# Moving eight node units from the diffusion stage into the first layer's sums, and five sum places per turn instead of four

## The chip, the cores and the metric

One NeuronCore of a Trainium2 chip runs the whole program, a single launch. The metric is device time in microseconds, the median over executions. TensorE (PE) multiplies, VectorE (DVE), ScalarE (ACT) and GpSimd (POOL) do the rest; SyncE (SP), ACT and POOL issue the DMAs. POOL issues the gathers, that is DMAs whose rows in memory are picked by a list of indices.

## What is computed

Four graph layers in a row on 50000 nodes of 256 features and 12500 edges, each followed by a layer norm of input plus output:

```python
x = _layernorm(x + L0(x))   # two attention convolutions (GAT) with self loops
x = _layernorm(x + L1(x))   # graph transformer attention, only over edges
x = _layernorm(x + L2(x))   # gated message, out = agg + x, normed once more inside
x = _layernorm(x + L3(x))   # linear, silu, 6 steps of diffusion, linear

def _spmm(h, src, dst, inv_deg):
    return segment_sum(h[src], dst) * inv_deg[:, None]
for i in range(1, k + 1):             # k = 6
    term = _spmm(term, src, dst, inv_deg) / float(i)
    out = out + term
```

Only some nodes are the end of an edge. For all others the attention and message sums are empty, and the result of a node follows from its own row: a projection, norms, a linear layer with silu, a last linear layer and a norm. The kernel computes this *nodes' own path* for all 50000 nodes, in 196 units of 256 nodes, and the edge path overwrites the rows of the nodes that edges end in.

## The kernel before

**Edge path.** The edges are sorted by their end node and lie in T = 100 tiles of 128 slots. The stages follow one another: `project1`, `softmax`, `gat1`, `gather_out1`, `softmax`, `gat2`, `project_qkv`, `softmax`, `attend`, `mlp`, `diffuse`, `output`. Each opens a block in which every engine has a program of its own, and engines wait for one another by semaphores. Nothing schedules: the order in the code is the order on each engine.

**`gat1`, the first layer's sums.** It runs over 50 pairs of tiles. For each pair k, SP loads an equality matrix `b_equal` and two tiles `b_x` (four buffers), DVE multiplies them by the scores (`weigh`, L1474, two instructions), PE sums by matmul with the equality matrix (L1461), DVE adds (`join`, L1487) and ACT stores the result to `out1` in memory. DVE's order is `weigh(i)`, `join(i-1)`. Before pair 1 it does four long instructions of dot products (L1492, L1495). POOL issues 53 small gathers (`get_rep`, `rep_i`) in a row and then waits for the stage's end.

**`Dense`, the nodes' own path.** A turn works on up to six units at different stages. Its parts are, with the lag in units behind the newest one: `project` on PE (L801, lag 0), `add_c12` on DVE (L848, 0), `square_u` on ACT (L686, 0), `var_1` on DVE (L706, L707, 0), `pow_1` on POOL (L745, 0), `scales` on ACT (L692, 1), `scale_shift` on DVE (L713, L715, L718, 2), `var_3` (L725, L727, 2), `pow_3` on POOL (L750, 2), `third_norm` on DVE (L735, 2), `transpose` on PE (L678, 3), `move_x3` on ACT (L699, 3), `hidden` on PE (L810, 3), `silu` on ACT (L829, 4), `out_project` on PE (L819, 4), `add_out` on DVE (L855, L857, 4), `square_w` on ACT (L835, 5), `var_5` (L861, 5), `pow_5` on POOL (L868, 5), `last_norm` on ACT (L841, 5), load (L785) and store (L792) on SP. A stage with n units takes n + 5 turns. Within a turn each engine passes a few *gaps*, the same number on each engine, in which a stage puts work of its own. `PIECES`, the number of gaps, is 4.

**Where the units stand.** 36 units (`early`) run in `gather_out1` with tiles `m_...`; the other 160 run in `diffuse` with tiles `n_...`, in 165 turns with 660 gaps.

**`diffuse`.** Six steps of 100 sums and a closing one. `places` gives each step a sixth of the gaps and puts its 100 sums over all but the last nine of them, and the closing sum five gaps before the end. For a sum, POOL gathers 128 rows of `h` (`i_messages`, L620), eight sums ahead; PE multiplies by the equality matrix (L2558) in the sum's gap; DVE scales and adds (L2595) one gap later; SP stores the result to `h` two gaps later (five buffers `i_y`). After a step's last sum, SP loads the tiles' end rows (L2493), PE and DVE do the closing sum (L2554, L2589), POOL scatters it (L2526), and only then may POOL gather for the next step.

Of the kernel before, what the change touches and what calls it, by code (L numbers as in the profile page):

```python
# [90 lines left out]
class Net:  # L91
# [4 lines left out]
    def __init__(self, nc, a, ctx, edge_ctx):  # L96
# [3 lines left out]
        self.R = R = T * P  # L100
        self.early = 36
        self.H, self.DE = 8, a["edge_attr_t"].shape[0]
# [650 lines left out]
class Dense(Unmet):  # L753
# [117 lines left out]

    PIECES = 4

    def turn_sp(self, sp, j, u, gap):
        if v := self.at(j, u, -2):
            self.load(sp, *v)
        gap()
        gap()
        if v := self.at(j, u, 5):
            self.store(sp, *v)  # L880
        gap()
        gap()

    def turn_pe(self, pe, j, u, gap):
        if v := self.at(j, u, 0):
            self.project(pe, *v)
        gap()
        if v := self.at(j, u, 3):
            self.transpose(pe, *v)
        gap()  # L890
        if v := self.at(j, u, 4):
            self.out_project(pe, *v)
        gap()
        if v := self.at(j, u, 3):
            self.hidden(pe, *v)
        gap()

# [14 lines left out]
    def turn_dve(self, dve, j, u, gap):  # L912
# [14 lines left out]
        if v := self.at(j, u, 4):  # L927
            self.add_out(dve, *v)
        if third:
            self.third_norm(dve, *third)  # L930
        gap()

    def turn_gp(self, gp, j, u, gap):
        gap()
        gap()
        if v := self.at(j, u, 5):
            self.pow_5(gp, *v)
        if v := self.at(j, u, 2):
            self.pow_3(gp, *v)
        if v := self.at(j, u, 0):  # L940
            self.pow_1(gp, *v)
        gap()
        gap()
# [444 lines left out]
def gat1(net):  # L1388
# [7 lines left out]
    N = T // G  # L1396
    with Stage(nc) as st:
        EQ = st.sb("b_equal", [P, G, P], n=NB)
        X = st.sb("b_x", [P, G, 2, D], n=NB)
# [14 lines left out]
        block = st.ctx.enter_context(nc.Block())  # L1414

        @block.sync
        def _(sp):
            def load(k):
                if k < N:
# [3 lines left out]
                    sp.dma_start(X[k % NB][:, :, 0, :], tiles(net.out1[R:2 * R, :], k)).then_inc(x_in[k % NB], 16)  # L1423
                    sp.dma_start(X[k % NB][:, :, 1, :], net.proj_dst[k * G:(k + 1) * G, :, :].rearrange("g p d -> p g d")).then_inc(x_in[k % NB], 16)
            for k in range(N):
                load(k)

        @block.scalar
        def _(act):
            for k in range(N):  # L1430
                act.wait_ge(o_ready, k + 1)
                act.dma_start(net.ends[k * G:(k + 1) * G, :, :].rearrange("g r d -> r g d"), O[k % 3][0:2, :, :]).then_inc(ends_out[k % 3], 16)
                act.dma_start(tiles(net.out1, k), O[k % 3][:]).then_inc(stored[k % 3], 16)
            for u in range(3):
                act.wait_ge(ends_out[u], 16 * len(range(u, N, 3)))
# [3 lines left out]
        def _(gp):  # L1439
            for t in range(*net.ROWS):  # L1440
                get_rep(net, t).then_inc(reps_in, 16)
            gp.wait_ge(o_ready, N + 1)
# [8 lines left out]
        def _(pe):  # L1451
            for k in range(N + 1):
# [4 lines left out]
                else:  # L1457
                    pe.wait_ge(eq_in[k % NB], 16 * (k // NB + 1))
                    pe.wait_ge(msg_ready, k + 1)
                    for g in range(G):  # L1460
                        mm = nc.tensor.matmul(sums[k % 2][:, g * D:(g + 1) * D], EQ[k % NB][:, g, :], M[k % 2][:, g, 0, :], start=True, stop=True)  # L1461
                    mm.then_inc(summed, 1)

        @block.vector
        def _(dve):
# [30 lines left out]
            for i in range(1, N):  # L1496
                weigh(i)
                join(i - 1)
            join(N - 1)
            dve.wait_ge(reps_in, 16 * (net.ROWS[1] - net.ROWS[0]))  # L1500
# [4 lines left out]
def gather_out1(net):  # L1505
# [3 lines left out]
    with Stage(nc) as st:  # L1509
        dn = Dense(net, st.ctx, "m", 0, net.early)  # L1510
        dn.banks(*st.ps("m_bank", 4))
# [932 lines left out]
def diffuse(net):  # L2444
# [8 lines left out]
    with Stage(nc) as st:  # L2453
        dn = Dense(net, st.ctx, "n", net.early, Dense.all_units(net) - net.early)
        dn.banks(*st.ps("n_bank", 4))
# [362 lines left out]
```

## Time and profile before

| what | us |
|---|---|
| median of 3 runs (4128.31 to 4131.36) | 4131.34 |
| the profiled execution | 4160.81 |
| its span, first to last instruction | 4159.1 |
| its mean granted TensorE clock | 0.901 of full |

| engine | busy us | share |
|---|---|---|
| PE | 3324.5 | 80% |
| DVE | 2815.1 | 68% |
| POOL | 2545.2 | 61% |
| ACT | 1860.4 | 45% |

Busy time counts no instruction that only issues a DMA from SP or ACT, waits or branches. In this trace `gat1` runs from about 633 to 811 us, `gather_out1` from 811 to about 1120, `diffuse` from 2571 to about 3943. A line of the trace's order in time has start, duration, engine, line, operation, tiles (written <- read), shapes, how many instructions of one kind it merges, and in brackets how long the engine stood idle before it and what ended that. The names of tiles are the program's; the prefix `s_b_` is `gat1`, `m_` is `gather_out1`, `s_i_` and `n_` are `diffuse`.

### The profile page before, as it was taken

The numbers are of one execution on the slowest core, as the hardware profiler recorded it, in microseconds if no ns is written. First come the engines' busy times: TensorE is split into PE (matmuls) and PEld (weight loads), VectorE is DVE, ScalarE is ACT, GpSimd is POOL, SyncE is SP. The second block draws the span as 40 slices with busy tenths as digits, with TensorE's granted clock in tenths as the row PEclk, the third lists the DMA queues.
The fourth block names the chain that finished last, engine by engine and source line by source line (L and its number), as shares of the span: only waits on it lengthen the run. The fifth ranks groups of instructions, "written<-read, shape, count | busy, mean of one in ns | idle before, by whom it ended". The sixth has DMA issues, their size and how long they took to land. (4 is left out here: it accounts for less than half of the span.)

```text
span 4159.1 us, 57942 instructions
## 1 busy us (share of the span) xinstructions
PE 3324.5 (80%) x14668; PEld 2594.7 (62%) x14668; DVE 2815.1 (68%) x7889; ACT 1860.4 (45%) x5076; POOL 2545.2 (61%) x2930
## 2 busy tenths in 40 slices
PE   4999924568677699856999995499999999999775
PEld 3888712357455455433777774387878787878654
DVE  4666645559778455586666663488888888888732
ACT  2777700047523222223333331266656666666554
POOL 4777665188567566523333331487878787878667
PEclk8999955679899899955999997699999999999998
DMA  4877707724267322256333334976767676767664
GB/s 111 236 236 237 232 9 222 243 79 129 84 194 206 91 78 77 61 155 191 90 113 109 115 115 131 298 235 202 234 197 235 201 234 198 235 201 235 186 197 156
DMA packets 709256, 705.57 MB, mean 170 GB/s; under 512 B 92630, under 2 KB 663049, under 8 KB 708702
## 3 DMA queue, kind: packets, MB, share of 16 engines
q1 hardware_dynamic: 604546, 478.91, 37.5%
q0 software_dynamic: 74752, 181.57, 15.5%
q10 hardware_dynamic: 29660, 41.70, 3.0%
q8 instruction: 115, 1.88, 0.2%
q14 instruction: 183, 1.50, 0.1%
HBM read 422.60 MB, written 296.47 MB: 173 GB/s over the span
## 5 line engine op out<-in xcount | busy, mean ns | idle before, releaser
L620 POOL DMA_INDIRECT s_i_messages<-h,table_row x600 | 647.0, 1078 | 191.5 <-issue 129.7
L2558 PE MATMUL s_i_bank<-s_i_messages,s_i_equal 128*128 128x256 f32 x1200 | 364.5, 387 | 81.4 <-DMA s_i_messages<-h,table_row 76.8
L801 PE MATMUL s_n_bank<-w,n_xt 128*128 128x256 f32 x1280 | 308.0, 384 | 20.5 <-DMA n_xt<-in_x_t 20.5
L2595 DVE SCALAR_TENSOR_TENSOR s_i_y<-s_i_bank,s_i_scale,s_i_acc 128x256 f32<-128x256 f32 x600 | 284.6, 475 | 44.6 <-PE s_i_bank L2558 23.5
L819 PE MATMUL s_n_bank<-w_out,n_ht 128*128 128x256 f32 x1280 | 307.8, 384 | 0.9 <-ACT n_ht L829 0.9
L810 PE MATMUL s_n_bank<-n_x3t,w_in 128*128 128x256 f32 x1280 | 305.0, 381 | 0.0
L2558 PEld LDWEIGHTS s_i_bank<-s_i_messages,s_i_equal 128*128 128x128 f32 x1200 | 218.8, 193 | 112.7 <-issue 82.5
L841 ACT ACTIVATE n_w<-n_w,n_small 128x256 f32<-128x256 f32 x320 | 145.5, 502 | 313.0 <-POOL n_small L868 277.8
L801 PEld LDWEIGHTS s_n_bank<-w,n_xt 128*128 128x128 f32 x1280 | 247.2, 193 | 55.9 <-DMA n_xt<-in_x_t 20.9
L819 PEld LDWEIGHTS s_n_bank<-w_out,n_ht 128*128 128x128 f32 x1280 | 246.1, 193 | 35.6 <-ACT n_ht L829 1.3
L810 PEld LDWEIGHTS s_n_bank<-n_x3t,w_in 128*128 128x128 f32 x1280 | 244.6, 191 | 33.8 <-ACT n_x3t L699 0.2
L620 POOL DMA_INDIRECT s_e_x<-x,s_e_i x200 | 196.1, 981 | 111.0 <-issue 97.6
L620 POOL DMA_INDIRECT s_a_x<-in_x,index x200 | 200.2, 1001 | 64.2 <-issue 54.2
L735 DVE TENSOR_SCALAR n_x<-n_z,n_small 128x256 f32<-128x256 f32 x320 | 118.1, 409 | 121.4 <-POOL n_small L750 106.1
L2162 POOL TENSOR_TENSOR s_g_small<-s_g_small,neg_half 128x2 f32<-128x2 f32 (+1 forms) x51 | 43.7, 856 | 247.7 <-DVE s_g_small L2405 247.7
L686 ACT ACTIVATE n_squares<-n_u 128x256 f32<-128x256 f32 x320 | 130.6, 410 | 143.2 <-DVE n_u L848 79.1
L745 POOL TENSOR_TENSOR n_small<-n_small,neg_half 128x4 f32<-128x4 f32 x160 | 165.0, 1031 | 42.4 <-DVE n_small L707 42.4
L1855 PE MATMUL s_e_ps_qv<-w_qv,s_e_xt 128*128 128x512 f32 x400 | 189.9, 597 | 0.0
L692 ACT ACTIVATE n_z<-gamma_bc,n_small 128x256 f32<-128x256 f32 x320 | 173.3, 591 | 13.7 <-POOL n_small L745 13.7
L1461 PE MATMUL s_b_sums<-s_b_messages,s_b_equal 128*128 128x256 f32 x200 | 87.9, 586 | 106.1 <-DVE s_b_messages L1474 82.7
L2397 DVE SCALAR_TENSOR_TENSOR s_g_y<-s_g_x,real,s_g_bank 128x512 f32<-128x512 f32 x50 | 37.4, 747 | 184.1 <-PE s_g_bank L2253 184.1
L868 POOL TENSOR_TENSOR n_small<-n_small,neg_half 128x2 f32<-128x2 f32 x160 | 116.5, 728 | 72.2 <-DVE n_small L861 68.7
(422 smaller groups left out, 9436.1 us busy)
## 6 DMA issues: line engine op xcount, KB each, us to landing
h<-s_i_y SPq DMA_DIRECT2D x600, 128.0 KB
n_xt<-in_x_t SPq DMA_DIRECT2D x160, 256.0 KB
out<-n_w SPq DMA_DIRECT2D x160, 256.0 KB
s_i_equal<-eq_tab SPq DMA_DIRECT2D x600, 64.0 KB
x<-s_x_rows SPq DMA_DIRECT2D x100, 256.0 KB
out<-s_a_hs SPq DMA_DIRECT2D x100, 128.0 KB
proj_dst<-s_a_hd SPq DMA_DIRECT2D x100, 128.0 KB
h<-s_h_rows SPq DMA_DIRECT2D x50, 256.0 KB
```

What stands on the lines that cost most here:

```text
L620: return net.nc.gpsimd.indirect_dma_start(out, None, table, bass.IndirectOffsetOnAxis(index, 0))
L686: sq = self.nc.scalar.activation(self.squares[0][:, g, :], self.U[u][:, g, :], ACT.Square, scale=self.D ** -0.5, accum_out=self.S[u][:, g: ...
L692: sc = self.nc.scalar.activation(self.Z[u][:, g, :], self.net.bc["gamma"][:], ACT.Identity, bias=self.S[u][:, self.POWERED + g:self.POWERE ...
L735: nm = self.nc.vector.tensor_scalar(self.X3[u][:, g, :], self.Z[u][:, g, :], s[:, 24 + 2 * g:25 + 2 * g], s[:, 32 + g:33 + g], ALU.subtrac ...
L745: self.nc.gpsimd.tensor_tensor(self.S[u][:, first:first + n], self.S[u][:, 8 - n:8], self.net.neg_half[:, 0:n], ALU.pow).then_inc(self.sca ...
L801: mm = self.nc.tensor.matmul(self.pr[:, g * self.D:(g + 1) * self.D], self.XT[u][:, c, g * P:(g + 1) * P], self.net.w12[:, c, :], start=c ...
L810: mm = self.nc.tensor.matmul(self.hd[:, 2 * m * P:2 * (m + 1) * P], self.net.w_in[:, c, m * P:(m + 1) * P], self.X3T[:, c, :], start=c == ...
L819: mm = self.nc.tensor.matmul(self.op[:, g * self.D:(g + 1) * self.D], self.HT[:, m, g * P:(g + 1) * P], self.net.w_out[:, m, :], start=m = ...
L841: nm = self.nc.scalar.activation(self.W[u][:, g, :], self.W[u][:, g, :], ACT.Copy, scale=self.S[u][:, 40 + g:41 + g])
L1855: nc.tensor.matmul(qvs[b][:, :], XT[b][:, c, :], net.w_qv[:, c, :], start=c == 0, stop=c == C - 1)
L2558: nc.tensor.matmul(banks[r % 4][:, 0:D], EQ[q % NM][:], M[q % NM][:], start=True, stop=True).then_inc(summed, 1)
L2595: V.scalar_tensor_tensor(Y[q % NY][:], banks[r % 4][:, 0:D], scale[:, s, t:t + 1], acc[:, t, :], ALU.mult, ALU.add).then_inc(added, 1)
```

## The change

Eight units become a third `Dense` with tiles `l_...` in `gat1`; `gather_out1` keeps its 36 and starts with unit 8; `diffuse` keeps 152, in 157 turns. `PIECES` becomes 5, so `diffuse` has 785 gaps and `gather_out1` 205 instead of 164. In `gat1` the 13 turns of the eight units stand behind every third pair, k = 0, 3, ..., 36, and the 53 small gathers on POOL are split into 13 chunks, one ahead of each turn.

```diff
-        self.early = 36
+        self.first_units, self.early = 8, 36
...
-    PIECES = 4
+    PIECES = 5
...  # turn_pe: a second gap behind hidden
             self.hidden(pe, *v)
+        gap()
         gap()
...  # turn_dve: a gap between add_out and third_norm
             self.add_out(dve, *v)
+        gap()
         if third:
             self.third_norm(dve, *third)
...  # turn_gp and turn_sp: a third gap at their end
+        gap()
         gap()
         gap()
...  # gat1
+        dn = Dense(net, st.ctx, "l", 0, net.first_units)
+        dn.banks(*st.ps("l_bank", 4))
+        TURNS = dn.units + 5
+        EVERY = (N - 1) // TURNS
...
+        def turn_at(k):
+
+            i = k // EVERY
+            return (i // 2, i % 2) if k % EVERY == 0 and 0 <= i < TURNS else None
...  # SP
             for k in range(N):
                 load(k)
+                if v := turn_at(k - 3):
+                    dn.turn_sp(sp, *v, none)
...  # ACT, behind the two stores of pair k
+                if v := turn_at(k):
+                    dn.turn_act(act, *v)
...  # POOL
-            for t in range(*net.ROWS):
-                get_rep(net, t).then_inc(reps_in, 16)
+            t0, t1 = net.ROWS
+            at = lambda i: t0 + min(i, TURNS) * (t1 - t0) // TURNS
+            for i in range(TURNS):
+                for t in range(at(i), at(i + 1)):
+                    get_rep(net, t).then_inc(reps_in, 16)
+                dn.turn_gp(gp, i // 2, i % 2, none)
...  # PE, behind the matmuls of pair k
+                    if v := turn_at(k):
+                        dn.turn_pe(pe, *v, none)
...  # DVE
                 weigh(i)
                 join(i - 1)
+                if v := turn_at(i - 1):
+                    dn.turn_dve(dve, *v, none)
...
-        dn = Dense(net, st.ctx, "m", 0, net.early)
+        dn = Dense(net, st.ctx, "m", net.first_units, net.early)
...
-        dn = Dense(net, st.ctx, "n", net.early, Dense.all_units(net) - net.early)
+        dn = Dense(net, st.ctx, "n", net.first_units + net.early, Dense.all_units(net) - net.first_units - net.early)
```

What that moves, first on DVE in `gat1`. `s4_b_...` are the stage's own tiles. Before, the two kinds of instruction alternate from the dot products to the end:

```order
L1495 TENSOR_REDUCE dots2<-s4_b_products 128x200
L1474 TENSOR_TENSOR s4_b_messages1<-s4_b_x1,scores_1 128x512 x2
L1487 TENSOR_TENSOR s4_b_out0<-s4_b_sums0,s4_b_messages0 128x512
L1474 TENSOR_TENSOR s4_b_messages0<-s4_b_x2,scores_1 128x512 x2
L1487 TENSOR_TENSOR s4_b_out1<-s4_b_sums1,s4_b_messages1 128x512
```

After, on DVE in the middle of the stage:

```order
L1517 TENSOR_TENSOR s4_b_out0<-s4_b_sums1,s4_b_messages1 128x512
L713 TENSOR_TENSOR l_z1<-l_u1,l_z1 128x512
L715 TENSOR_TENSOR l_z1<-l_z1,beta_bc 128x512
L718 BN_STATS l_small1<-l_z1 128x6 x2
L848 TENSOR_TENSOR l_u1<-s4_l_bank0,c12 128x512
L861 TENSOR_SCALAR l_small0<-l_small0 128x2
L725 BN_AGGR l_small1<-l_small1 128x2 x2
L727 TENSOR_SCALAR l_small1<-l_small1 128x2
L706 TENSOR_SCALAR l_small1<-l_small1 128x2
L707 TENSOR_SCALAR l_small1<-l_small1 128x2
L855 TENSOR_TENSOR l_w1<-s4_l_bank3,l_x31 128x512
L857 TENSOR_TENSOR l_w1<-l_w1,b_out_bc 128x512
```

A whole turn now stands behind the addition of every third pair (the last of it, L735, follows these rows), and the next pair's multiplication stands behind the turn.

On DVE in `diffuse`, the end of one turn and the start of the next, before:

```order
L2595 SCALAR_TENSOR_TENSOR s12_i_y1<-s12_i_bank0,s12_i_scale,s12_i_acc 128x256
L855 TENSOR_TENSOR n_w0<-s12_n_bank3,n_x30 128x512
L857 TENSOR_TENSOR n_w0<-n_w0,b_out_bc 128x512
L735 TENSOR_SCALAR n_x30<-n_z0,n_small0 128x256 x2
L2595 SCALAR_TENSOR_TENSOR s12_i_y2<-s12_i_bank1,s12_i_scale,s12_i_acc 128x256
L713 TENSOR_TENSOR n_z1<-n_u1,n_z1 128x512
```

After, in a turn whose place between L857 and L735 is one of those without a sum:

```order
L2627 SCALAR_TENSOR_TENSOR s12_i_y2<-s12_i_bank3,s12_i_scale,s12_i_acc 128x256
L855 TENSOR_TENSOR n_w1<-s12_n_bank3,n_x31 128x512
L857 TENSOR_TENSOR n_w1<-n_w1,b_out_bc 128x512
L735 TENSOR_SCALAR n_x31<-n_z1,n_small1 128x256 x2
L2627 SCALAR_TENSOR_TENSOR s12_i_y3<-s12_i_bank0,s12_i_scale,s12_i_acc 128x256
L713 TENSOR_TENSOR n_z0<-n_u0,n_z0 128x512
```

Most turns still hold four sums; which of the five places stays empty wanders through the turn.

## Rows read from the trace of the kernel before

**Rows 1.** Busy time by stretch: us, busy (count) by engine, granted clock, DMA share, GB/s.

```profile
706.00:800.00 94.00, 59.71 (x134) 34.58 (x134) 65.36 (x108) 0.00 (x0) 0.18 (x1) 0.65 0.96 318
...
2680.00:3930.00 1250.00, 1174.76 (x5562) 994.59 (x5561) 1076.63 (x2941) 769.32 (x2351) 1006.98 (x1052) 0.99 0.72 219
```

**Rows 2.** Groups on POOL, 2680 to 3930: busy us, mean ns | idle before, releasers.

```profile
L620 POOL DMA_INDIRECT s_i_messages<-h,table_row x575 | 621.9, 1081 | 167.0 <-issue 123.5 <-DVE n_small L727 28.1 <-DMA h<-s_i_bound,bound_row 10.2
L745 POOL TENSOR_TENSOR n_small<-n_small,neg_half 128x4 f32<-128x4 f32 x156 | 160.9, 1031 | 0.0
L868 POOL TENSOR_TENSOR n_small<-n_small,neg_half 128x2 f32<-128x2 f32 x158 | 115.1, 728 | 68.7 <-DVE n_small L861 65.3
```

**Rows 3.** POOL in order of time, one turn of the diffusion with four sums.

```profile
3100.81 0.72 POOL L868 TENSOR_TENSOR n_small<-n_small,neg_half 128x2 f32<-128x2 f32 x1
...
3103.38 1.50 POOL L620 DMA_INDIRECT s_i_messages<-h,table_row  x1 [0.18 <-issue]
3105.19 0.96 POOL L620 DMA_INDIRECT s_i_messages<-h,table_row  x1 [0.31 <-issue]
3106.45 0.95 POOL L620 DMA_INDIRECT s_i_messages<-h,table_row  x1 [0.30 <-issue]
...
3108.69 0.72 POOL L868 TENSOR_TENSOR n_small<-n_small,neg_half 128x2 f32<-128x2 f32 x1
```

**Rows 4.** PE in order of time: a sum in that turn, and neighbours without sums.

```profile
3103.54 0.60 PE L2558 MATMUL s_i_bank<-s_i_messages,s_i_equal 128*128 128x256 f32 x2
3103.97 1.89 PE L819 MATMUL s_n_bank<-w_out,n_ht 128*128 128x256 f32 x8
...
2847.11 1.89 PE L810 MATMUL s_n_bank<-n_x3t,w_in 128*128 128x256 f32 x8
2848.83 0.38 PE L801 MATMUL s_n_bank<-w,n_xt 128*128 128x256 f32 x1
```

**Rows 5.** DVE in order of time, the end of that turn.

```profile
3102.26 0.73 DVE L735 TENSOR_SCALAR n_x<-n_z,n_small 128x256 f32<-128x256 f32 x2 [0.66 <-POOL n_small L750]
3102.91 0.48 DVE L2595 SCALAR_TENSOR_TENSOR s_i_y<-s_i_bank,s_i_scale,s_i_acc 128x256 f32<-128x256 f32 x1
3103.30 0.68 DVE L713 TENSOR_TENSOR n_z<-n_u,n_z 128x512 f32<-128x512 f32 x1
```

**Rows 6.** POOL in order of time: the first gather of a new step.

```profile
2852.24 1.00 POOL L620 DMA_INDIRECT s_i_messages<-h,table_row  x1 [2.00 <-DMA h<-s_i_bound,bound_row]
```

**Rows 7.** Groups on DVE in `gat1`, 633 to 800.

```profile
L1474 DVE TENSOR_TENSOR s_b_messages<-s_b_x,scores 128x512 f32<-128x512 f32 x100 | 64.9, 690 | 66.1 <-DMA s_b_x<-proj_dst 61.2 <-issue 3.6
L1487 DVE TENSOR_TENSOR s_b_out<-s_b_sums,s_b_messages 128x512 f32<-128x512 f32 x50 | 34.3, 686 | 26.1 <-DMA proj_dst<-s_a_hd 14.6 <-PE s_b_sums L1461 11.5
L1495 DVE TENSOR_REDUCE dots<-s_b_products 128x200 f32<-128x1600 f32 x2 | 5.7, 2856 | 0.1
L1492 DVE TENSOR_TENSOR s_b_products<-scores 128x1600 f32<-128x1600 f32 x2 | 3.6, 1822 | 0.0
```

**Rows 8.** DVE in order of time in `gat1`: the first pair, a long wait, the last pair.

```profile
637.61 1.29 DVE L1474 TENSOR_TENSOR s_b_messages<-s_b_x,scores 128x512 f32<-128x512 f32 x2 [41.65 <-DMA s_b_x<-proj_dst]
...
705.10 0.69 DVE L1487 TENSOR_TENSOR s_b_out<-s_b_sums,s_b_messages 128x512 f32<-128x512 f32 x1 [7.29 <-DMA proj_dst<-s_a_hd]
...
793.05 0.69 DVE L1487 TENSOR_TENSOR s_b_out<-s_b_sums,s_b_messages 128x512 f32<-128x512 f32 x1 [1.63 <-PE s_b_sums L1461]
```

**Rows 9.** ACT in order of time, one turn of the diffusion.

```profile
3110.26 0.82 ACT L829 ACTIVATE n_ht<-s_n_bank,cols 128x256 f32<-128x256 f32 x2
3111.61 0.60 ACT L699 ACTIVATE n_x3t<-s_n_bank 128x512 f32<-128x512 f32 x1 [0.53 <-PE s_n_bank L678]
3112.11 1.08 ACT L692 ACTIVATE n_z<-gamma_bc,n_small 128x256 f32<-128x256 f32 x2
3113.09 0.41 ACT L835 ACTIVATE n_squares<-n_w 128x256 f32<-128x256 f32 x1
...
3114.39 0.42 ACT L686 ACTIVATE n_squares<-n_u 128x256 f32<-128x256 f32 x1 [0.40 <-issue]
```

**Rows 10.** PE in `gather_out1`, in order of time, after an idle stretch of 5.72 us.

```profile
895.10 3.62 PE L819 MATMUL s_m_bank<-w_out,m_ht 128*128 128x256 f32 x8
```

More of the change, by code:

```diff
@@ L941, in turn_gp @@
             self.pow_1(gp, *v)
+        gap()
         gap()
@@ L1414, in gat1, with none @@
         block = st.ctx.enter_context(nc.Block())
+        def none():
+            pass
+        def turn_at(k):
+            i = k // EVERY
+            return (i // 2, i % 2) if k % EVERY == 0 and 0 <= i < TURNS else None
         @block.sync
@@ L1424, in load @@
                     sp.dma_start(X[k % NB][:, :, 1, :], net.proj_dst[k * G:(k + 1) * G, :, :].rearrange("g p d -> p g d")).then_inc(x_in[k % NB], 16)
+            for u in range(2):
+                dn.load(sp, 0, u)
             for k in range(N):
                 load(k)
+                if v := turn_at(k - 3):
+                    dn.turn_sp(sp, *v, none)
+            for u in range(2):
+                sp.wait_ge(dn.stored[u], 16 * (dn.units // 2))
         @block.scalar
```

## The prediction

> **What bounds the kernel now.** I read busy time by stretch first, then who waits for whom in the two stages that change, then single turns in order of time.
>
> In the middle of the diffusion PE is busy for 1174.76 of 1250 us, at clock 0.99 [rows 1]. That looks like the bound, and it is not, since matmul records overlap. Matmul groups L810 and L801 that follow each other without a sum start 1.73 us apart, and a sum takes 0.43 (3103.54 to 3103.97) [rows 4]. With four sums and transposes that take about as long as a sum, PE needs 3 x 1.73 + 5 x 0.43 = 7.35 us a turn. The turn takes 7.88 (3100.81 to 3108.69) [rows 3].
>
> POOL is full there. Each gather starts 1.26 after the one before (3105.19 to 3106.45), and the 0.30 between them is ended by nothing but issue [rows 3]. Four gathers are 5.04 us; what is left of the turn, 2.84, goes to the three powers and to a first gather that takes 1.50 instead of 0.95 [rows 3]. DVE waits 0.66 for POOL ahead of L735 [rows 5]. Over the stretch POOL idles beyond issue for about 68.7 + 10.2 us, nearly all between steps [rows 2]. So POOL sets the turn, and a turn costs 1.26 per gather plus 2.84.
>
> In `gat1` nothing of this holds: DMA is busy for 0.96 at 318 GB/s, POOL for 0.18 us of 94, and the clock is 0.65 [rows 1]. DVE has the longest chain, from 637.61 to 793.05 plus 0.69, 156 us [rows 8]. Of these 64.9 + 34.3 + 5.7 + 3.6 = 108.5 are work [rows 7], and 47.5 are waits, mostly for loads and stores; the longest, up to 7.29 each, fall while the 53 small gathers run [rows 8].
>
> **The diffusion, part by part.** Eight turns go. The 600 gathers stay, so what POOL saves is 8 x 2.84 = 22.7 us, and not eight whole turns of 7.88 (63 us). Five places only let the same sums stand in fewer turns: 100 sums over 121 or 122 gaps are 4.1 a turn. POOL then needs 4.1 x 1.26 + 2.84 = 8.0, PE 5.62 + 4.1 x 0.43 = 7.4; POOL stays the bound.
>
> The new place ahead of L735 stands in DVE's wait: an addition occupies 0.39 (3102.91 to 3103.30) of 0.66 [rows 5], so it costs nothing. If that cover were gone it would cost at most 0.39 in each of some 146 turns (six steps of 24.4), 57 us.
>
> Between steps, POOL may gather again only when the closing sum is scattered (2.00 us of wait at the end of that chain [rows 6]). Seven gaps lie between the last sum and the scatter. They are 1.75 turns before and 1.4 after, 0.35 x 5.6 = 2 us less if the turn sets them, nothing if the DMAs do. About half, 1 us at each of five boundaries: -5. The first 100 us of the stage (bulk loads) and its last turns wait for DMAs; I leave them as they are.
>
> What a first gather of 1.50 costs beyond 0.95 coincides with L713, which starts at 3103.30, while the gather starts at 3103.38 [rows 3, 5]. In turns whose last place is empty (about one in five), L713 starts 0.39 earlier and the overlap shrinks: 146 / 5 x 0.35 = 10 us at most, nothing at least; I take -1. Sum for the diffusion: -22.7 - 5 - 1 = -29; bounds -23 and -43 (and +28 if the cover were gone).
>
> The Trainium skill ("SBUF — State Buffer", Who interferes with whom) says that a DVE instruction with two SBUF inputs contends with a GpSimd instruction that reads SBUF, and that order of issue decides who blocks. L713 has two such inputs and the row of 1.50 agrees. By that rule alone, the empty last place would shift the block to the power L745 in part, and the sum would be -28 instead of -29.
>
> **`gat1`, part by part.** The added work on DVE is that of eight units. In the diffusion a turn of DVE takes 7.88 less 0.66 of wait less four additions of 0.39, 5.66. Eight of them are 45 us. That is the least it can cost if nothing is waited for inside a turn, and if all of it went into the 47.5 of waits, the stage would take no longer at all.
>
> I do not expect that, since here the turn stands between two pairs, and its parts wait for one another across engines. ACT starts its turn when the pair is joined and its two stores are issued (0.73 after). Then it does silu, 0.8, `move_x3`, 0.5, `scales`, 0.98, `square_w`, 1.0 or more, `square_u`, 0.94; starts of these are 3110.26, 3111.61, 3112.11, 3113.09 and 3114.39 [rows 9]. `var_1` on DVE needs the last and stands ahead of L855, L857 and L735 (2 x 0.72 + 0.73). So DVE's turn takes 0.73 + 4.3 + 0.2 + 2.2 = 7.4 after the pair, of which 1.7 is wait for ACT. Three turns of thirteen have all parts. The others by the same chain with the parts that they have: 3.0, 2.9, 4.7, 5.1, 6.3 ahead of them and 6.9, 5.9, 4.6, 4.2, 1.9 behind. All thirteen: 22.2 + 22.0 + 23.5 = 68 us.
>
> PE adds to that while its clock is low. A group of eight records took 3.62 instead of 1.89 in `gather_out1` behind an idle stretch of 5.72 [rows 4, 10]. PE's turn at 1.2 GHz would be 11.2 us instead of 5.6, and the next pair's sum stands behind it: up to 4 us more a turn, 10 turns, 40. At full clock nothing. The stage's 0.65 lies near 1.2 GHz, but a turn fills PE for over 5 us; I take 9 us. The Trainium skill ("TensorE: Matmul & The Clock Gate", Part 1) has the clock go to full once PE has been busy for a while and back when it idles. This speaks for the smaller value; by it the sum would be 3 to 5 us lower.
>
> Waits for DMA: the 13 pairs behind the last turn still run at the DMA's pace, 94 us for some 38 pairs or 2.45 each against 1.98 of work, 6 us. In a turn SP stands at the unit's store until `last_norm`, and the loads of the fourth pair ahead are queued behind it; these land about when DVE wants them, so 0 to 1 us in eight turns, 4. The long waits during the small gathers go, since those now come in fours.
>
> DVE's chain: 108.5 + 68 + 9 + 10 = 195.5 against 156, **+39**; bounds +5 and +75.
>
> `gather_out1`: same units, same turns, same gathers. Its 40 small gathers fill 8 turns instead of 10, POOL-bound in both; 0, between -3 and +3.
>
> Profiled execution: 4160.8 + 39 - 29 + 2 (the stage waits for the last unit store at its end, which no row shows) = 4172.8. The median of the runs is 29.5 us below the profiled execution. I carry the difference over: 4131.3 + 12 = **4143**.
>
> **The rivals.** (a) *The units fill the waits.* If ACT and PE run far enough ahead, DVE's turn costs its 5.66 and takes the place of the DMA waits: 108.5 + 45 + 12 = 166, +10. With -29 and +2 this is 4114. For it: 47.5 us of waits and idle ACT, POOL. Against: ACT's part can't start before the join. It decides as soon as a full turn on DVE is under 6.2 us. (b) *The diffusion gets no shorter*, because something other than POOL binds at five places: the five `i_y` buffers come back too late, or PE does. Then -7 instead of -29: 4165. Against: PE has 0.5 us of room a turn. (c) *`gat1` stays at 1.2 GHz*, or SP's store starves the loads: +69 instead of +39, 4173. (d) *The first gather's stall goes away in all turns*, since DVE's order changed. Then PE binds at 7.4 to 7.8 in some 80 turns: some 25 us more, 4118. Against: the distance from L745 to L713 changes in one turn of five alone.
>
> **How the numbers follow.** Forecast 0.56, own range 4130 to 4158. (a) 0.16, (b) 0.10, (c) 0.10, (d) 0.08. A measurement of this kernel tells a change from none at about 0.2%, 8.3 us, so from 4123.1 to 4139.6 counts as the same. The forecast's lower part lies there: 0.16 of its 0.56, and 0.40 slower. (a) gives 0.13 faster and 0.03 same, (d) 0.05 and 0.03; (b) and (c) are slower. Faster 0.18, same 0.22, slower 0.60. The range takes in (a), (d) and most of (b) and (c): 4112 to 4173.
>
> **What would show it.** In the diffusion: step period 4 to 5 us shorter, a turn with four sums still 7.9, POOL's gathers still ended by issue alone, DVE's wait ahead of L735 near 0.3 where its new place is filled. In `gat1`: DVE's chain near 195, a full turn near 7.4 with waits for ACT ahead of L861 and L706, waits for loads under 15 us in all. Clock above 0.65. The prediction falls if a full turn on DVE is near 5.7 (a), if the step period stays (b), if PE's records there are mostly over 0.6 us (c), or if four-sum turns are 7.4 (d).

## The result, and the profile after

| | before | after |
|---|---|---|
| median, us | 4129.83 (4 runs, 4127.78 to 4131.36) | 4160.80 (4 runs, 4158.44 to 4164.26) |
| the profiled execution, us | 4160.81 | 4158.44 |
| `gat1` with `project1` ahead of it, start to start | 751.0 | 783.2 |
| `gather_out1` | 332.8 | 336.2 |
| `diffuse` | 1379.9 | 1353.2 |

The changed kernel is slower: ratio 1.0076 with an interval of 1.0059 to 1.0093, +31 us. The forecast was 4143, +12. The profiled executions differ by -2.4 us only. So the traces and the medians don't tell the same story, and most of what follows is about that.

Busy time by stretch of the kernel after (columns as in [rows 1]):

```profile
706.00:800.00 94.00, 63.45 (x215) 46.30 (x213) 64.57 (x127) 24.11 (x73) 43.05 (x42) 0.81 0.75 238
2680.00:3930.00 1250.00, 1156.30 (x5410) 977.02 (x5411) 1047.62 (x2861) 736.18 (x2252) 992.11 (x1039) 0.98 0.74 221
```

In `gat1` the clock rose from 0.65 to 0.81, and DMA fell from 0.96 to 0.75: the stage is no longer at the pace of its transfers. Now DVE in order of time: the first pair, a turn with all its parts at pair 21, and the last pair.

```profile
631.91 1.29 DVE L1504 TENSOR_TENSOR s_b_messages<-s_b_x,scores 128x512 f32<-128x512 f32 x2 [47.22 <-DMA s_b_x<-proj_dst]
...
722.46 0.69 DVE L1517 TENSOR_TENSOR s_b_out<-s_b_sums,s_b_messages 128x512 f32<-128x512 f32 x1
...
725.87 0.69 DVE L848 TENSOR_TENSOR l_u<-s_l_bank,c 128x512 f32<-128x512 f32 x1 [0.61 <-PE s_l_bank L801]
729.02 0.17 DVE L861 TENSOR_SCALAR l_small<-l_small 128x2 f32<-128x2 f32 x1 [2.46 <-ACT l_squares L835]
...
731.94 1.28 DVE L1504 TENSOR_TENSOR s_b_messages<-s_b_x,scores 128x512 f32<-128x512 f32 x2
733.14 0.68 DVE L1517 TENSOR_TENSOR s_b_out<-s_b_sums,s_b_messages 128x512 f32<-128x512 f32 x1
...
825.86 0.69 DVE L1517 TENSOR_TENSOR s_b_out<-s_b_sums,s_b_messages 128x512 f32<-128x512 f32 x1 [1.63 <-PE s_b_sums L1489]
```

The chain that [rows 8] show as 156 us long is 825.86 + 0.69 - 631.91 = 194.6 us; forecast 195.5. A pair without a turn takes 2.0 us from one L1517 to the next; from pair 21 to 22 it is 733.14 - 722.46 = 10.68, so this turn costs 8.7. The two other turns with all parts (pairs 15 and 18) cost 6.8 and 6.7. The three make 7.4 on average, the number of the forecast, but that 7.4 was for full clock, with PE's slow clock as a surcharge of its own; at full clock the turn is 6.8, so 0.6 less than forecast. Pair 21 is dearer because PE ran it at 1.2 GHz (granted clock 0.50 from 722 to 726): its L801 group took 3.62 us instead of 1.89, and DVE waited for it at L848, and for ACT, which had waited for PE, at L861. PE in order of time:

```profile
722.21 3.62 PE L801 MATMUL s_l_bank<-w,l_xt 128*128 128x256 f32 x8
```

What DVE waited for in the whole stage, in groups (window 600 to 850, so L1504 includes the 47.22 ahead of the first pair):

```profile
L1504 DVE TENSOR_TENSOR s_b_messages<-s_b_x,scores 128x512 f32<-128x512 f32 x100 | 64.7, 688 | 61.1 <-DMA s_b_x<-proj_dst 58.4
L1517 DVE TENSOR_TENSOR s_b_out<-s_b_sums,s_b_messages 128x512 f32<-128x512 f32 x50 | 34.3, 686 | 3.0 <-PE s_b_sums L1489 2.9
L855 DVE TENSOR_TENSOR l_w<-s_l_bank,l_x 128x512 f32<-128x512 f32 x8 | 5.5, 688 | 5.8 <-PE s_l_bank L819 5.8
L861 DVE TENSOR_SCALAR l_small<-l_small 128x2 f32<-128x2 f32 x8 | 1.4, 170 | 14.9 <-ACT l_squares L835 14.9
L706 DVE TENSOR_SCALAR l_small<-l_small 128x2 f32<-128x2 f32 x8 | 1.4, 170 | 6.3 <-ACT l_squares L686 6.3
```

Behind the first pair 61.1 - 47.2 = 13.9 us of waits for loads are left, where [rows 7] had 66.1 - 41.7 = 24.4 and another 26.1 ahead of the additions. In their place stand 14.9 + 6.3 for ACT and 5.8 for PE inside the turns.

In the diffusion, POOL in order of time, a turn with four sums:

```profile
3123.45 1.00 POOL L745 TENSOR_TENSOR n_small<-n_small,neg_half 128x4 f32<-128x4 f32 x1
3124.63 1.50 POOL L620 DMA_INDIRECT s_i_messages<-h,table_row  x1 [0.18 <-PE s_i_bank L2590]
3126.43 0.95 POOL L620 DMA_INDIRECT s_i_messages<-h,table_row  x1 [0.30 <-issue]
3127.70 0.95 POOL L620 DMA_INDIRECT s_i_messages<-h,table_row  x1 [0.30 <-issue]
3128.95 0.96 POOL L620 DMA_INDIRECT s_i_messages<-h,table_row  x1 [0.30 <-DVE n_small L727]
...
3132.50 1.50 POOL L620 DMA_INDIRECT s_i_messages<-h,table_row  x1 [0.18 <-issue]
```

The turn takes 3132.50 - 3124.63 = 7.87 (7.88 in [rows 3]), and the gathers are still 1.25 to 1.27 apart. From the middle of one step to that of the next it is 214.4 us instead of 218.8, mean of five: 4.4 shorter.

### The profile page after: what moved, and what is told of

Same layout as the page of the kernel before. It is cut to its first block and busy times, and to the rows that moved or that the text cites. A ratio compares the mean times of both kernels' runs of the same rounds, so it can differ in the third digit from the quotient of the medians.

```text
span 4156.7 us, 57935 instructions
## 1 busy us (share of the span) xinstructions
PE 3314.6 (80%) x14668; PEld 2598.4 (63%) x14668; DVE 2812.0 (68%) x7889; ACT 1857.7 (45%) x5076; POOL 2540.2 (61%) x2930
## 5 line engine op out<-in xcount | busy, mean ns | idle before, releaser
L620 POOL DMA_INDIRECT s_i_messages<-h,table_row x600 | 633.8, 1056 | 196.0 <-issue 104.2
L2590 PE MATMUL s_i_bank<-s_i_messages,s_i_equal 128*128 128x256 f32 x1200 | 351.9, 389 | 76.0 <-DMA s_i_messages<-h,table_row 71.5
L801 PE MATMUL s_n_bank<-w,n_xt 128*128 128x256 f32 x1216 | 296.6, 388 | 20.6 <-DMA n_xt<-in_x_t 20.6
L819 PE MATMUL s_n_bank<-w_out,n_ht 128*128 128x256 f32 x1216 | 296.0, 388 | 0.1
L810 PE MATMUL s_n_bank<-n_x3t,w_in 128*128 128x256 f32 x1216 | 289.3, 381 | 0.3 <-ACT n_x3t L699 0.3
L801 PEld LDWEIGHTS s_n_bank<-w,n_xt 128*128 128x128 f32 x1216 | 237.2, 195 | 55.5 <-DMA n_xt<-in_x_t 21.1
L620 POOL DMA_INDIRECT s_e_x<-x,s_e_i x200 | 193.6, 968 | 110.9 <-POOL s_e_i L1866 78.7
L819 PEld LDWEIGHTS s_n_bank<-w_out,n_ht 128*128 128x128 f32 x1216 | 234.4, 195 | 32.6 <-ACT n_ht L829 0.5
L810 PEld LDWEIGHTS s_n_bank<-n_x3t,w_in 128*128 128x128 f32 x1216 | 232.8, 192 | 33.0 <-ACT n_x3t L699 0.7
L620 POOL DMA_INDIRECT s_a_x<-in_x,index x200 | 195.8, 979 | 64.7 <-issue 55.9
L735 DVE TENSOR_SCALAR n_x<-n_z,n_small 128x256 f32<-128x256 f32 x304 | 112.1, 409 | 115.8 <-POOL n_small L750 115.8
L745 POOL TENSOR_TENSOR n_small<-n_small,neg_half 128x4 f32<-128x4 f32 x152 | 155.0, 1020 | 45.9 <-DVE n_small L707 45.9
L620 POOL DMA_INDIRECT s_d_x<-in_x,index x100 | 98.4, 984 | 95.5 <-DVE s_d_y L1817 48.4
L868 POOL TENSOR_TENSOR n_small<-n_small,neg_half 128x2 f32<-128x2 f32 x152 | 116.8, 769 | 60.8 <-DVE n_small L861 57.5
```

What stands on the lines that cost most here:

```text
L620: return net.nc.gpsimd.indirect_dma_start(out, None, table, bass.IndirectOffsetOnAxis(index, 0))
L745: self.nc.gpsimd.tensor_tensor(self.S[u][:, first:first + n], self.S[u][:, 8 - n:8], self.net.neg_half[:, 0:n], ALU.pow).then_inc(self.sca ...
L801: mm = self.nc.tensor.matmul(self.pr[:, g * self.D:(g + 1) * self.D], self.XT[u][:, c, g * P:(g + 1) * P], self.net.w12[:, c, :], start=c ...
L810: mm = self.nc.tensor.matmul(self.hd[:, 2 * m * P:2 * (m + 1) * P], self.net.w_in[:, c, m * P:(m + 1) * P], self.X3T[:, c, :], start=c == ...
L819: mm = self.nc.tensor.matmul(self.op[:, g * self.D:(g + 1) * self.D], self.HT[:, m, g * P:(g + 1) * P], self.net.w_out[:, m, :], start=m = ...
L868: self.nc.gpsimd.tensor_tensor(s[:, 40:42], s[:, 38:40], self.net.neg_half[:, 0:2], ALU.pow).then_inc(self.dev5, 1)
```

## The experiments

The runs fell on several chips, and these are of two kinds for this program: on some the kernel before takes 4125 to 4131 us (medians), on two others 4156 ("at 4155" below), at about the same granted clock (0.895 to 0.910 in all runs). Each chip was used on one occasion only, so whether the chip or the occasion makes the difference isn't shown; "chip" stands for both. The result above is of the first kind. Each ratio below is against the kernel before on the same chip. By "the chain of `gat1`" I mean the time from the first multiplication to the end of the last addition on DVE, as above.

Where the expectations number their theories: theory 1 says that the long waits of `gat1` in [rows 8] are not in the executions that were timed; the others are told where they stand.

### The kernel before, once more (chip at 4155)

> The kernel before, unchanged, profiled a second time. Question: the first profiled execution was 29.5 us over the median of the plain runs, the profiled execution of the changed kernel is not. Theory 1 (the long waits in gat1 beside the small gathers are not there in every execution): this one comes out near 4130 us, gat1 near 130 to 140 us on DVE instead of 156. Theory 2 (the excess is spread over all stages): near 4130 with gat1 still at 156, and each other stage a little shorter. Theory 3 (a profile of this kernel costs 30 us): again 4160.

Profiled execution 4161.43, medians of its neighbours 4155.68. The chain of `gat1` is 158.0 us, and the long waits are there as in [rows 8] (up to 10.5 us from one addition to the next). Here the profile agrees with the medians, so "the profiler makes it 30 us longer" falls. It says nothing on the chips of the other kind.

### The parts of the change, one at a time (chip at 4155)

`gat1` alone; the eight units are computed there and a second time in the old place:

```diff
-        self.early = 36
+        self.first_units, self.early = 8, 36
...  # gat1 as in the changed kernel; m and n units and PIECES as before
```

> The kernel before, with the eight units in gat1 as in the changed kernel, while gather_out1 keeps units 0 to 35 and diffuse the other 160 (so eight units are computed twice) and PIECES stays 4. It prices gat1's part alone. My sum: +39 us, bounds +5 to +75. Theory 1 of b_again (timed runs have a shorter gat1 than the profile showed): +55 to +60. Rival (the units fill waits): +10.

Ratio 1.0085 (1.0066 to 1.0105), +35 us; `gat1` is 41.9 us longer in the trace. Near the forecast of +39.

The five places alone:

```diff
-    PIECES = 4
+    PIECES = 5
...  # and the gaps in turn_pe, turn_dve, turn_gp, turn_sp
```

> The kernel before with five places in a turn and no unit moved: 165 turns in diffuse, 825 gaps. It prices the places alone. POOL-bound: each turn costs 2.84 plus 1.26 a gather whatever the places, so the time changes by what the step's ends save, 0 to -5 us. Rival (the DVE or PE order costs or gains by itself): beyond -15 or +15.

Ratio 0.9996 (0.9983 to 1.0010): nothing. The steps are 218.7 us long, as before. So the places themselves neither help nor cost in sum, and the -5 for the step ends isn't seen in the time. Inside, things move all the same: over the 500 gathers from the middle of the first step to the middle of the last, POOL's gathers are 17 us shorter than before and its three powers 21 us longer, in 138 turns instead of 137.

The changed kernel with `gat1` as before; units 0 to 7 are computed nowhere, so this kernel leaves out the own path of 2048 nodes (chip at 4155):

```diff
-        dn = Dense(net, st.ctx, "l", 0, net.first_units)
...  # and its turns; the 53 small gathers in a row again
```

> The changed kernel with gat1 as before: units 0 to 7 are computed nowhere, diffuse has 152 units and five places. It leaves out eight units, so it prices what diffuse gets back in timed runs. My sum: -29 us (POOL 8 x 2.84 plus the step ends). If each unit were worth a whole turn: -63. If the diffusion got no shorter: 0 to -7.

Ratio 0.9935 (0.9909 to 0.9960), -27 us, with an interval from -38 to -17. In the traces `diffuse` alone is 23.6 us shorter. This is what the diffusion gives, and the sum said -29.

### The changed kernel on a chip at 4155

> The changed kernel, unchanged, beside the kernel before on the chip of these runs. If the parts simply add, gat1 +35 to +40 (e_gat1_units_only) and diffuse -26 (the two profiles), it comes to +10 to +15 us. If the first result holds on any chip, +24 to +38.

4170.91 (11 runs) against 4155.66 (23 runs): ratio 1.0037 (1.0023 to 1.0051), **+15 us**, near the forecast +12, and not the +31 of the result. The chain of `gat1` is 195.3 us, so it is as long as on the other kind of chip. The changed kernel is 10 us slower here than in the result, the kernel before 26; what makes the two differences unequal must lie in the kernel before.

### Does POOL set the turns of the diffusion?

```diff
         # pow_5
+        self.nc.gpsimd.tensor_tensor(s[:, 44:46], s[:, 38:40], self.net.neg_half[:, 0:2], ALU.pow)
```

> The changed kernel with pow_5 on POOL done twice in every turn, the first into unused columns. If POOL sets the diffusion's turns, a turn gets 0.7 us longer wherever POOL is full: 0.7 x about 135 turns of diffuse, +95 us, step period 214 to 230. If PE sets them, POOL's extra work is hidden: +0 to +15.

POOL in order of time (L869 is the second power):

```profile
3118.87 0.73 POOL L868 TENSOR_TENSOR n_small<-n_small,neg_half 128x2 f32<-128x2 f32 x1
3119.58 0.69 POOL L869 TENSOR_TENSOR n_small<-n_small,neg_half 128x2 f32<-128x2 f32 x1
...
3122.09 1.51 POOL L620 DMA_INDIRECT s_i_messages<-h,table_row  x1 [0.18 <-issue]
...
3130.61 1.50 POOL L620 DMA_INDIRECT s_i_messages<-h,table_row  x1 [0.18 <-issue]
```

A turn is 3130.61 - 3122.09 = 8.52 instead of 7.87: the added 0.69 comes through nearly whole. Steps are 230.8 us long, the diffusion is 92.4 us longer than in the changed kernel on that chip, and `gather_out1` 14.9. This is one execution, 4287.66: +117 against the median of the changed kernel, +108 against its profiled execution. The +95 expected is met by the diffusion alone. POOL is the bound there, though PE is busy for 92% of the middle of the stage. In `gather_out1` its 41 turns would make 28 us if all came through, and about half did, so POOL sets only a part of that stage.

### What a turn in `gat1` costs

The next pair's multiplication is put into the turn, behind `scale_shift`, where DVE otherwise waits for ACT:

```diff
+                    def gap():
+                        nonlocal weighed
+                        if next(n) == 0 and i + 1 < N:
+                            weigh(i + 1)
+                            weighed = i + 1
-                    dn.turn_dve(dve, *v, none)
+                    dn.turn_dve(dve, *v, gap)
```

> The changed kernel with one thing moved: in gat1 DVE does the next pair's weigh (1.3 us) inside the turn, behind scale_shift, instead of behind the turn, so that it fills the wait for ACT ahead of var_5 and var_1. Theory (a full turn costs 7.4 or more because DVE waits for ACT and PE inside it): 1.0 to 1.3 us less in each of eleven turns, -11 to -15 us against a_again. Rival (gat1 is bound by loads or by SP's stores): no change against a_again, waits for loads take the place.

Ratio 1.0033 (1.0015 to 1.0050), the same as the changed kernel on that chip, where 11 to 15 us less were expected. The edit did what it should, and its groups on DVE (window 633 to 845) show what took its place:

```profile
L1504 DVE TENSOR_TENSOR s_b_messages<-s_b_x,scores 128x512 f32<-128x512 f32 x100 | 64.6, 688 | 69.4 <-DMA s_b_x<-proj_dst 67.1
...
L861 DVE TENSOR_SCALAR l_small<-l_small 128x2 f32<-128x2 f32 x8 | 1.3, 166 | 1.1 <-ACT l_squares L835 0.9
```

The wait for ACT at L861 fell from 14.5 us (the changed kernel on that chip) to 1.1. But the waits for loads behind the first pair grew from 58.6 - 44.3 = 14.3 to 69.4 - 44.3 = 25.1. The chain is 193.0 instead of 195.3. Why the loads are late is in SyncE's waits; here those of the changed kernel in the first run (columns: who waited <- for whom: us in total, times, longest):

```profile
SPq L792 <- ACT l_w L841: 55.9, 8, 9.6
SPq L1437 <- PE s_b_sums L1489: 31.1, 19, 5.8
```

SP stands in the stores of the eight units (L792) for 55.9 us, and the loads for the pairs are queued behind them. Two kernels take that away, the second with the edit above too (chip at 4125):

```diff
-                if v := turn_at(k - 3):
+                if v := turn_at(k - 4):
                     dn.turn_sp(sp, *v, none)
```

> The changed kernel with one edit: in the first layer's sums SP does its part of a turn (a unit's load and the store of a finished unit) one pair later, that is behind the loads of the fourth pair ahead and not ahead of them. Nothing else moves. In the trace of the changed kernel SP stands for 54 us in eight such stores, up to 8.6 us each, with the loads queued behind them; DVE waits about 14 us for loads behind the first pair. Theory (DVE's turn with its waits for ACT sets the pace, the loads come second): the waits for loads fall by some 5 us, gat1 is 0 to 6 us shorter, the time 0 to 6 us below the changed kernel, that is 9 to 15 us above the kernel before. Rival (SP's stores starve the loads, and that is most of what a turn costs): 14 us or more below the changed kernel.

> Both edits: the next pair's multiplication stands inside the turn on DVE, and SP's part of the turn stands one pair later. With the first edit alone a turn became 1 to 1.5 us shorter in the trace, yet waits for loads grew from about 14 to 25 us and the time did not move. Theory (the gain of the first edit was given back as waits for loads, because SP stands in the unit's store with the loads queued behind it): now waits for loads fall back to about 10 us, gat1 is some 12 to 16 us shorter than in the changed kernel, the time -1 to +5 us against the kernel before. Rival (the loads are late because the DMA engines are full and not because SP issues them late): waits for loads stay near 25, the time stays near +14.

The store alone: ratio 1.0076 (1.0061 to 1.0091), which is what the changed kernel had in the result, on a chip of this kind; waits for loads behind the first pair 9.7 us, chain 193.6. Both edits: 1.0050 (1.0035 to 1.0065), 10 us less on the same chip; the waits for loads are 13.0 where the first edit alone had 25.1, the one at L861 is 3.4, the chain is 185.2. So the two waits cover each other, and only taking both away pays. The changed kernel itself was not run on this chip, and each single edit on one kind only, so this rests on ratios from several chips; on one chip alone it is shown that the multiplication inside the turn gives 10 us once the store is moved, and on another that it gives nothing without that. The absolute numbers of both expectations are missed: the store alone +32.7 against the kernel before where 9 to 15 were expected, both +22.5 where it was -1 to +5, since on this kind of chip the changed kernel starts from +31; I had carried +15 over. Against the changed kernel `gat1`'s chain is 9 us shorter with both edits, where 12 to 16 were expected.

### The long waits of `gat1` without the units

The kernel before, with the small gathers in 13 chunks, each behind the sums of every third pair:

```diff
-            for t in range(*net.ROWS):
-                get_rep(net, t).then_inc(reps_in, 16)
+            for i in range(13):
+                gp.wait_ge(summed, 3 * i + 1)
+                for t in range(t0 + i * (t1 - t0) // 13, t0 + (i + 1) * (t1 - t0) // 13):
+                    get_rep(net, t).then_inc(reps_in, 16)
```

> The kernel before, with the 53 small gathers of gat1 in 13 chunks, each waiting for the sum of every third pair, and no unit. If the small gathers cause gat1's long waits in the timed runs, -15 to -25 us. If the timed runs have no such waits, 0 within 0.2%.

On the chip at 4155: 4137.79, ratio 0.9960 (0.9944 to 0.9975), **-17 us**, the chain 136.7 instead of 158.0. This beats both kernels there. The changed kernel has this pacing in it as a side effect, so there its +15 hides a gain of some 17 in `gat1`. Then the same again, with a trace of the kernel before, on a chip that gave 4125.94:

> The kernel before, unchanged, once more, with its trace. Its median was 4130 where the changed kernel came out 31 us slower, 4125 on a third occasion, and 4155 where the changed kernel was only 15 us slower; both of its traces so far (4161 each) are of the slower kind. Chips differ, and the question is which stage of the kernel before is shorter on a quicker one. Theory 1: where the kernel before runs at 4125 to 4131, its long waits in gat1 (up to 9 to 11 us between additions while the 53 small gathers run) are missing, so gat1 ends some 15 us earlier behind its first pair, at about 125 to 130 us from the first to the last addition instead of 144. Rival: the waits are there as ever (143 to 146 us), and the difference of 30 us lies in the stages that read and write whole tables (project1 458 instead of 467, mlp and others). Where the chip gives about 4155 again, this run tells nothing new.

> The kernel before with the 53 small gathers of gat1 in 13 chunks, each behind the sums of every third pair, as in the run that came out 17 us quicker, on the same chip as the look at the kernel before. Where the chip gives the kernel before about 4155: again 13 to 20 us quicker. Where it gives 4125 to 4131: by theory 1 within 5 us of the kernel before, since the waits that the pacing takes away aren't there; by the rival 13 to 20 us quicker as well, about 4110.

Paced: 4124.34 (12 runs) against 4125.94 (17 runs), ratio 0.9996 (0.9984 to 1.0007). Nothing left to gain, and the trace of the kernel before says why. Busy time by stretch, first before on the chip at 4155 (the first repetition), then before on this one:

```profile
675.00:712.00 37.00, 10.77 (x21) 6.37 (x22) 10.60 (x17) 0.00 (x0) 23.93 (x25) 0.50 0.46 138
```

```profile
675.00:698.00 23.00, 15.89 (x37) 9.53 (x36) 17.00 (x27) 0.00 (x0) 17.88 (x17) 0.65 1.10 366
675.00:712.00 37.00, 25.74 (x59) 15.06 (x57) 27.85 (x45) 0.00 (x0) 18.82 (x18) 0.66 1.10 368
```

In the first the DMA engines are busy for 0.46 at 138 GB/s and DVE for 10.60 us; on the second they run at 1.10 and 368 GB/s. There the small gathers end at 698 already, but until then POOL issues them at the same pace, and the DMA engines move 366 GB/s beside them. In order of time, all engines, first a long wait of the first:

```profile
699.15 1.29 DVE L1474 TENSOR_TENSOR s_b_messages<-s_b_x,scores 128x512 f32<-128x512 f32 x2
...
700.59 2.05 PE L1461 MATMUL s_b_sums<-s_b_messages,s_b_equal 128*128 128x256 f32 x4 [7.06 <-issue]
...
708.85 0.36 SPq L1421 DMA_DIRECT2D s_b_equal<-eq_tab  x1
708.86 0.69 DVE L1487 TENSOR_TENSOR s_b_out<-s_b_sums,s_b_messages 128x512 f32<-128x512 f32 x1 [8.41 <-DMA proj_dst<-s_a_hd]
```

The name in the bracket misleads: `proj_dst<-s_a_hd` is a store of `project1`, the last of which was issued at 514.6. SP's load L1421 waits for nothing but PE's sum, and it and the addition start together. The semaphore that PE raises at the end of the sum goes up at 708.83, 6.8 us after the start of the pair's last matmul (702.01); in a pair without a long wait it takes 0.65. So what DVE, and SP with it, waits for here is PE's sum being reported as done. It is so in each of the four traces with long waits, wherever the semaphore is recorded: up to 7.6 us instead of 0.65, and the addition starts 0.03 later. And the transfers aren't what is slow. The loads issued by 699.27 have landed by 702.61, and then the DMA engines have next to nothing to do until SP issues again:

```profile
702.70:708.80 6.10, 0.00 (x0) 0.00 (x0) 0.00 (x0) 0.00 (x0) 2.83 (x3) 0.50 0.05 11
```

Now the ends of the chain of the second, where no addition is more than 3.0 us behind the one before it:

```profile
626.98 1.29 DVE L1474 TENSOR_TENSOR s_b_messages<-s_b_x,scores 128x512 f32<-128x512 f32 x2 [44.22 <-DMA s_b_x<-proj_dst]
...
762.25 0.69 DVE L1487 TENSOR_TENSOR s_b_out<-s_b_sums,s_b_messages 128x512 f32<-128x512 f32 x1 [1.36 <-PE s_b_sums L1461]
```

The chain of `gat1` is 762.25 + 0.69 - 626.98 = 136.0 us, where [rows 8] have 156.1. Theory 1 holds for this chip, the only one at 4125 to 4131 with a trace of the kernel before; for the others of the kind it is inferred from their medians.

## Why the forecast was right in sign and short in size

The direction came out, and so did most terms of the sum; the size was +12 for +31. The 4160.8 measured lies outside the forecast's own range (4130 to 4158) and inside the wide one (4112 to 4173), where it is nearer to rival (b), 4165, and to (c), 4173, than to the forecast, though neither of their mechanisms was found. That it fell into the wide range is no proof of the reasons. By the prediction's own steps:

**POOL bounds the turn of the diffusion.** Right. 7.87 for four sums, and 0.69 more on POOL is 0.65 more a turn.

**The diffusion, -29.** Measured -26.7 between the two profiled executions, -27.1 against the trace from the chip at 4125, -24.8 between two chips at 4155, and -27 in medians with the units left out. The 8 x 2.84 = 22.7 is 3.8 a step; steps are 4.4 shorter. The -5 for the step ends was too much: what is left over is 0.6 x 5 = 3 at best, and nothing with the places alone. The cover of the added place held. DVE, in a turn that has an addition there:

```profile
3061.21 0.47 DVE L2627 SCALAR_TENSOR_TENSOR s_i_y<-s_i_bank,s_i_scale,s_i_acc 128x256 f32<-128x256 f32 x1
3061.95 0.74 DVE L735 TENSOR_SCALAR n_x<-n_z,n_small 128x256 f32<-128x256 f32 x2 [0.26 <-POOL n_small L750]
```

0.26 of wait is left of 0.66 [rows 5]; forecast 0.3. The term for the first gather's stall, -1, was too small. By the Trainium skill ("SBUF — State Buffer", Who interferes with whom) a DVE instruction with two SBUF inputs and a GpSimd instruction that reads SBUF contend. The rows agree in so far as the block moved in part from a gather to a power: over 500 gathers (middle of the first step to middle of the last) the gathers fell from 540.0 to 529.2 us, while L868 rose from 728 to 768 ns each, some 5 us in 131 turns. In the same stretch POOL's wait ahead of the five scatters grew from 6.9 to 16.2 us, and its wait ahead of L868 fell from 61.5 to 51.8. So the -27 is near the -29 in part because such pieces cancel.

**`gat1`, the chain of 195.5.** Measured 194.6, and 195.3 on the other kind of chip. That it is so near is in part luck, for two misses cancel: the 13 turns cost 97.5 - 13 x 2.0 = 71.5 us, against 68 + 9 + 4 = 81, and the 36 pairs without a turn lose 84.6 - 36 x 2.0 = 12.6 us, against 6. The cause of the full turn's length, the wait for ACT inside it, is right; its size at full clock is 6.8 and not 7.4. The 2 us for the last unit store at the stage's end, which no row showed, aren't there: from the last addition to the next stage it is 17.9 us before and 18.0 after. And the waits of before, "mostly for loads and stores", were in the long ones waits for PE's sum, as shown above; the term did not depend on it.

**`gather_out1`, 0 (±3).** +2.8 to +4.1; a little over, not followed further.

**The step that failed is the base.** "From 637.61 to 793.74, 156 us" was taken for the kernel whose median was 4131, and the 29.5 us between the profiled execution and the median were carried over as if they belonged to both kernels. They did not. The kernel before at 4125.9 has a chain of 136.0 and not 156.1: the long waits beside the small gathers are missing. The change paces the gathers, and so it takes those waits away where they are; where they are missing there is nothing to take. With 136.0, `gat1` is 195.5 - 136.0 = +59.5, the sum is 59.5 - 29 + 2 = +32.5, and the time 4163.8; measured 4160.8. Stage by stage against that trace: `gat1` +64.0, of which 4.9 lie ahead of its first multiplication (631.91 against 626.98), `gather_out1` +2.8, the stages between it and `diffuse` +7.7, `diffuse` -27.1, `output` -0.6, together +46.8. That is more than the medians' 31, since this one execution (4111.84) lies 14 below its neighbours' median.

On a chip at 4155 the same sum, base and all, gives +12, and +15 is measured. So one mechanism gives both numbers, within what single traces allow. That the profiled execution of before came from a chip of the slower kind is an inference: its 4160.81 lies outside all 33 runs on the others (4111.84 to 4137.08), and its waits are those of the repetition at 4155. The difference of 30 us between the kinds isn't `gat1`'s alone: of 49.6 us between the two traces of before, 22 are the chain, 11 lie ahead of it, nearly all in `project1`, and 15 between `gather_out1` and `diffuse`, 10 of them in `mlp`; why, is open.

**The rivals.** (a) fell: full turns cost 6.7 to 8.7, not 5.7. (b) showed no sign: the steps became shorter. The groups of DVE from 2680 to 3930 do have 19.1 us of waits for `i_y` stores after, and almost none before, but 17.1 of them are one wait at the stage's start, which the kernel before has too, just outside that window. DVE in order of time, before and after:

```profile
2662.97 0.48 DVE L2595 SCALAR_TENSOR_TENSOR s_i_y<-s_i_bank,s_i_scale,s_i_acc 128x256 f32<-128x256 f32 x1 [18.26 <-DMA h<-s_i_y]
```

```profile
2690.16 0.48 DVE L2627 SCALAR_TENSOR_TENSOR s_i_y<-s_i_bank,s_i_scale,s_i_acc 128x256 f32<-128x256 f32 x1 [17.14 <-DMA h<-s_i_y]
```

(c): the clock was 0.81 in the middle of `gat1`, so not 1.2 GHz throughout; SP's store does hold the loads back, hidden behind the wait for ACT. Where DVE's turn was made faster, the waits for loads grew by 11 us. (d) came true in few turns: of 114 turns with four sums (2680 to 3900), 55 took 7.80 to 7.95 us, 23 took 7.2 to 7.6, and 30 took 8.0 to 8.2. The median, 7.85, is that of before, where 116 of 127 lay at 7.80 to 7.95.

## What to carry to other kernels

Work put between two links of a chain costs its own chain of waits between engines, not its busy time: 6.7 to 8.7 us for a full turn here, where a turn adds 2.84 to the engine that bounds the diffusion. So eight units cost 59 us in one place to save 27 in the other. Before removing a wait, see what stands behind the next: the wait for ACT and the queue behind SP's store covered each other, and neither edit alone was worth anything that could be measured. The name of what ended a wait can mislead: see what else started at the same moment and what both wait for. A window with a fixed start can hold a wait in one trace and miss the same wait in the other. And a gap between the profiled execution and the medians is not an offset to be carried over: ask which stage it is in, above all when the change touches the stage with the longest irregular waits, and take a second trace of the kernel before if one can be had.

## What was not expected of the hardware

On the chips at 4155, 128-row gathers of single integers, issued by POOL every 1.25 us, went with a near standstill of the whole chain of `gat1`: in the trace shown four times in a row 5.8 to 10.5 us between additions, at 138 GB/s and a DMA share of 0.46. It began only behind the first half of the 53 gathers: in the same trace the DMA engines moved 363 GB/s from 664 to 675, with the gathers at the same pace. On the one chip of the other kind that left a trace, the same program at about the same clock ran through them at 366 GB/s. Pacing the gathers takes the waits away on the first and costs nothing on the second (-17 us, and 0). The transfers were not held back for want of DMA engines, which stood nearly idle: what came late was PE's report that its sum was done, and loads, additions and stores all hang on it. Why it comes late while small gathers run, and why on some chips only, was not found.

A gather on POOL that takes 1.50 instead of 0.95 us became rarer: over 1.3 us are 104 of 566 from 2700 to 3900, and 130 of 554 before. With the five places alone it is 68 of 553. The power L868 took 770 ns on average instead of 728 [rows 2], and 792 with the places alone.
